# Moving the rounding of the feed-forward weights from GpSimd to ScalarE in a gated cross-attention kernel

## The reference

```python
x = x + jnp.tanh(g_xattn[0]) * xattn(layernorm(x), ctx, Wq, Wk, Wv, Wo, bo)      # 8 batches, 224 x 750, 8 heads
h = gelu(jnp.einsum('nd,edh->neh', layernorm(x), w1) + b1, approximate=False)    # 8 experts, 512 -> 1024
y = jnp.einsum('neh,ehd->ned', h, w2) + b2                                       # 1024 -> 512
x = x + jnp.tanh(g_ffn[0]) * (y * norm_g[:, None, None]).sum(axis=1)             # norm_g from the gate, top 1
```

## Time and profile before

| | |
|---|---|
| Median of 3 runs | 1889.43 us (1887.07 to 1889.46) |
| The profiled execution | 1885.9 us, its span 1884.1 us |
| TensorE busy | 1821.5 us, 97% |
| VectorE busy | 1328.9 us, 71% |
| GpSimd busy | 1184.9 us, 63% |
| ScalarE busy | 812.7 us, 43% |
| Mean granted TensorE clock | 0.99 of full speed |
| Feed-forward part | about 1200 us, 64 steps |

### The profile page before, as it was taken

The page is one execution under the profiler, slowest core; times in us unless marked ns, Lnnn a source line. Parts: engine busy times, 40 slices in busy tenths (PEclk is TensorE's granted clock), DMA queues, the critical chain, the costliest instruction groups (busy, mean ns, idle before and its releaser), DMA issues.

```text
span 1884.1 us, 32919 instructions
## 1 busy us (share of the span) xinstructions
PE 1821.5 (97%) x10360; PEld 1647.3 (87%) x10360; DVE 1328.9 (71%) x2247; ACT 812.7 (43%) x1570; POOL 1184.9 (63%) x901
## 2 busy tenths in 40 slices
PE   6999999999999869999999999999999999999998
PEld 6999999999999758888888888887888888888887
DVE  6777777777776776766766667579766676676667
ACT  4767666766766543332323323233223233232322
POOL 5525354352544468877777777867777777777742
PEclk9999999999999979999999999999999999999999
DMA  5011111021110213121121211213311112112111
GB/s 174 17 32 59 34 37 55 21 67 29 42 43 13 81 33 122 62 67 56 56 67 45 67 56 56 68 53 116 106 50 62 59 53 67 55 56 66 46 46 51
DMA packets 51804, 110.38 MB, mean 59 GB/s; under 512 B 12953, under 2 KB 25241, under 8 KB 51745
## 3 DMA queue, kind: packets, MB, share of 16 engines
q1 hardware_dynamic: 51744, 109.63, 18.2%
HBM read 98.61 MB, written 11.01 MB: 58 GB/s over the span
## 4 chain that ended last, share of the span: by engine, by line
PE 85%; DVE 9%; issue 3%; ACT 3%; DMA 0%; DVEq 0%; ACTq 0%; SPq 0%
PE bank L683 30%; PE scores L658 28%; PE bank L537 15%; PE scores L601 4%; PE bank L611 4%; PE bank L624 4%; DVE xs L777 1%; DVE neg_max L860 1%; DVE queries L841 1%; ACT queries L1057 1%; DVE acc L944 1%; PE bank L544 1%; DVE probsT L777 0%; PE scores L719 0%; DVE values L777 0%
## 5 line engine op out<-in xcount | busy, mean ns | idle before, releaser
L683 PE MATMUL bank<-w2s,hs 128*128 128x512 f32 x2688 | 621.8, 390 | 5.0 <-DVE acc L944 5.0
L683 PEld LDWEIGHTS bank<-w2s,hs 128*128 128x128 f32 x2688 | 504.3, 188 | 109.5 <-DVE acc L944 7.0
L658 PE MATMUL scores<-xs,w1s 128*128 128x448 f32 x2688 | 562.1, 368 | 4.2 <-DVE h_sum L923 4.2
L658 PEld LDWEIGHTS scores<-xs,w1s 128*128 128x128 f32 x2688 | 507.5, 189 | 49.0 <-issue 2.8
L923 DVE TENSOR_TENSOR h_sum<-scores,h_sum 128x448 f32<-128x448 f32 x448 | 267.2, 620 | 192.2 <-PE scores L658 191.8
L944 DVE TENSOR_TENSOR acc<-bank,acc 128x512 f32<-128x512 f32 x434 | 295.8, 687 | 123.8 <-PE bank L683 114.6
L1183 ACT ACTIVATE h_full<-h_sum,b1T 128x448 f32<-128x448 f32 x256 | 170.9, 668 | 316.9 <-DVE h_sum L923 306.6
L777 DVE TENSOR_TENSOR hs<-h_full,hs 128x448 fp32r<-128x448 f32 x256 | 237.0, 926 | 50.6 <-ACT hs L1184 50.6
L1057 ACT ACTIVATE h_sum<-scores 128x448 f32<-128x448 f32 x64 | 34.9, 545 | 489.9 <-PE scores L658 489.8
L1244 POOL TENSOR_SCALAR probs<-probs,row_inv 112x750 f32<-112x750 f32 x64 | 140.5, 2195 | 164.4 <-DVE row_inv L866 164.4
L1339 POOL CAST w1s<-w_stage 128x768 fp32r<-128x768 f32 x64 | 68.6, 1072 | 182.9 <-PE scores L658 182.9
(11 more groups left out here) (112 smaller groups left out, 2123.8 us busy)
## 6 DMA issues: line engine op xcount, KB each, us to landing
w_stage<-in_L_ffn_w SPq DMA_DIRECT2D x128, 512.0 KB, 3.5
ctx_raw<-in_ctx SPq DMA_DIRECT2D x8, 752.0 KB, 4.6
ctx_raw<-in_ctx SPq DMA_DIRECT2D x7, 748.0 KB, 4.6
xa<-in_x SPq DMA_DIRECT2D x16, 224.0 KB, 2.7
xres<-in_x SPq DMA_DIRECT2D x16, 224.0 KB, 2.7
x_scratch<-xres SPq DMA_DIRECT2D x16, 224.0 KB, 2.3
xt_scratch<-yT SPq DMA_DIRECT2D x16, 224.0 KB, 2.9
x_raw<-xt_scratch SPq DMA_DIRECT2D x4, 896.0 KB, 6.1
```

The source lines that it names most:

```text
L658: mm = pe.matmul(mb[BANK_OF[name]][:, 0:TH], w1s[j % 2][:, s, W_OF[name], kc, :], xs[:, i, m, kc, :], start=n == 0, stop=n == 5)
L683: mm = pe.matmul(bank[:, :], hs[j % 2][:, s, ht, t * P:(t + 1) * P], w2s[j % 2][:, m, ht, :], start=n == 0, stop=n == 5)
```

## The change

The three roundings of a step's weights go to ScalarE: two of w1 (`round_w1`, part 0 of 768 columns and part 1 of 1024) and one of w2 (`round_w2`). Part 0 for the next step stands behind `keep_p1`, before the first GELU; part 1 for the next step and w2's rounding for this step stand at the end of the step, in (0, 7, 3) behind the seven `round_x`. GpSimd keeps the four sums and the three subtractions, and waits for the roundings with a new semaphore w1_hi and with w2_hi. In the last batch's plan ScalarE does items W0.1, W0.3, W1.1 and W1.3; w2's rounding for step (0, 0, 0) stands between the plan and step (0, 0, 1). Nothing changes for TensorE, VectorE and SyncE.

```diff
--- before.py
+++ after.py
@@ -276,6 +276,7 @@
         b1_loaded, b2_loaded = sem("b1_loaded"), sem("b2_loaded")
         small_loaded, small_set = sem("small_loaded"), sem("small_set")
         w1_loaded, w1_step, w1_split = sem("w1_loaded"), sem("w1_step"), sem("w1_split")
+        w1_hi = sem("w1_hi")
         w2_loaded, w2_hi, w2_split = sem("w2_loaded"), sem("w2_hi"), sem("w2_split")
         mix_psum, p1_out, sum_out = sem("mix_psum"), sem("p1_out"), sem("sum_out")
         h_hi, h_act, h_split = sem("h_hi"), sem("h_act"), sem("h_split")
@@ -1066,7 +1067,15 @@
                     copy(probs[0:QT, i, :], probs[0:QT, i, :],
                          scale=row_inv[0:QT, i:i + 1]).then_inc(probs_scaled[qt], 1)
                     return
-                if kind in "RMDLAWOBGZ":
+                if kind == "W":
+                    if item[3] in (1, 3):
+                        if item[2]:
+                            act.wait_ge(in_psum["P"], number(("P", 0, H - 1), B - 1))
+                        else:
+                            act.wait_ge(in_psum["P"], number(("P", 0, G - 1), B - 1))
+                        round_w1((0, 0, item[2]), item[3] // 2)
+                    return
+                if kind in "RMDLAOBGZ":
                     return
                 if kind == "N":
                     name, g = WEIGHT_PIECES[item[2]]
@@ -1184,6 +1193,28 @@
                 act.activation(hs[j % 2][:, 0, ht, half * TH:(half + 1) * TH], src, ACT.Gelu,
                                bias=bias).then_inc(h_act, 1)
 
+            def round_w1(g, part):
+
+                p, e, j = g
+                if part == 0:
+                    act.wait_ge(w1_loaded, upto(16, g, 16))
+                    if not early(g, 2):
+                        act.wait_ge(mix_psum, upto(NM, g, -NM))
+                    alone(act, passed["act"])
+                    copy(w1s[j % 2][:, 0, 0:3], w1_stage[:, 1:4]).then_inc(w1_hi, 1)
+                else:
+                    act.wait_ge(w1_step, upto(4, g, 4))
+                    alone(act, passed["act"])
+                    copy(w1s[j % 2][:, 0, 3:7], w1_stage[:, 4:8]).then_inc(w1_hi, 1)
+
+            def round_w2(g):
+                p, e, j = g
+                if not early(g, 2):
+                    act.wait_ge(y_psum, upto(NM, g, -NM))
+                act.wait_ge(w2_loaded, upto(16, g, 16))
+                alone(act, passed["act"])
+                copy(w2s[j % 2][:, 0], w2_stage[:, :, :]).then_inc(w2_hi, 1)
+
             def hidden(g, i):
                 if i == 0:
                     keep_p1(g)
@@ -1200,8 +1231,11 @@
             def step(g):
                 p, e, j = g
                 closing = isinstance(e, int) and e == NE - 1
+                after = following(g)
                 for i in range(NM):
                     hidden(g, i)
+                    if i == 0 and after:
+                        round_w1(after, 0)
                     if closing and j == 1 and i in (0, 2):
                         half = i // 2
                         act.wait_ge(gate_psum, 2 * p + half + 1)
@@ -1215,7 +1249,11 @@
                 if at(g, (0, NE - 1, JS - 1)):
                     for i in range(NM):
                         round_x(1, i)
-
+                if after:
+                    round_w1(after, 1)
+                round_w2(g)
+
+            round_w2((0, 0, 0))
             steps(act, step, (0, 0, 1))
 
 
@@ -1324,7 +1362,11 @@
                 raw, w = w1_stage, w1s[j % 2]
 
                 def after(n):
-                    pool.wait_ge(w1_step, upto(6, g, n))
+                    pool.wait_ge(w1_step, upto(4, g, n))
+                    alone(pool, passed["pool"])
+
+                def rounded(n):
+                    pool.wait_ge(w1_hi, upto(2, g, n))
                     alone(pool, passed["pool"])
 
                 if k == 0:
@@ -1333,23 +1375,17 @@
                     pool.tensor_tensor(raw[:, 4], raw[:, 0], raw[:, 3], ALU.add).then_inc(w1_step, 1)
                     pool.tensor_tensor(raw[:, 6], raw[:, 1], raw[:, 0], ALU.subtract).then_inc(w1_step, 1)
                 elif k == 1:
-                    if not early(g, 2):
-                        pool.wait_ge(mix_psum, upto(NM, g, -NM))
-                        alone(pool, passed["pool"])
-                    pool.tensor_copy(w[:, 0, 0:3], raw[:, 1:4]).then_inc(w1_step, 1)
                     after(1)
                     pool.tensor_tensor(raw[:, 5], raw[:, 4], raw[:, 1], ALU.subtract).then_inc(w1_step, 1)
                 elif k == 2:
                     after(3)
+                    pool.tensor_tensor(raw[:, 7], raw[:, 2], raw[:, 5], ALU.subtract).then_inc(w1_step, 1)
+                elif k == 3:
+                    rounded(1)
                     pool.tensor_tensor(w[:, 1, 0:3], raw[:, 1:4], w[:, 0, 0:3].bitcast(F32),
                                        ALU.subtract).then_inc(w1_split, 1)
-                    after(4)
-                    pool.tensor_tensor(raw[:, 7], raw[:, 2], raw[:, 5], ALU.subtract).then_inc(w1_step, 1)
-                elif k == 3:
-                    after(5)
-                    pool.tensor_copy(w[:, 0, 3:7], raw[:, 4:8]).then_inc(w1_step, 1)
                 else:
-                    after(6)
+                    rounded(2)
                     pool.tensor_tensor(w[:, 1, 3:7], raw[:, 4:8], w[:, 0, 3:7].bitcast(F32),
                                        ALU.subtract).then_inc(w1_split, 1)
 
@@ -1357,11 +1393,6 @@
 
                 p, e, j = g
                 w = w2s[j % 2]
-                if not early(g, 2):
-                    pool.wait_ge(y_psum, upto(NM, g, -NM))
-                pool.wait_ge(w2_loaded, upto(16, g, 16))
-                alone(pool, passed["pool"])
-                pool.tensor_copy(w[:, 0], w2_stage[:, :, :]).then_inc(w2_hi, 1)
                 pool.wait_ge(w2_hi, upto(1, g, 1))
                 alone(pool, passed["pool"])
                 pool.tensor_tensor(w[:, 1], w2_stage[:, :, :], w[:, 0].bitcast(F32), ALU.subtract).then_inc(w2_split, 1)
```

## The result

The changed kernel takes 1899.43 us (median of 5 runs, 1899.15 to 1899.96), the kernel before 1888.39 us on the same chip: 1.0059 times as long (95% interval 1.0044 to 1.0074), a loss of 11.0 us. The prediction was 1895.3 us, a loss of 5.9.

A forecast was written before the change was run, and what follows sets the result against it. The prediction took TensorE alone to set an ordinary step, 18.04 us. Gates -6.0, turn +11.6 and seam +0.3 summed to +5.9 on the median 1889.43: 1895.3 us, range 1888.5 to 1903.

The forecast's parts named there:

- the two stalls that were named: At the turn: TensorE waits 5.6 us for w2 before (0, 7, 3)'s tiles, 6.9 for w1 before (1, 0, 1)'s products.
- the third rival: Turn dearer at +14.1 by VectorE's x2 wait and low clock, gates -4 as w1 is late: 1899.8 us, chance 0.15.
- Ordinary steps, 0: The 60 ordinary feed-forward steps stay at 18.04 us, set by TensorE alone, and cost nothing.
- The margin of 2.9: In an ordinary step w1's low part ends at 15.1 us; TensorE asks for w1 at 18.04.
- Gate steps, -6.0 predicted: Steps (0, 7, 2) and (1, 7, 2) each gain 3.0 us as VectorE no longer meets GpSimd; bounds 3 and 6.2.
- the old collision: Gate step: VectorE's L1018 took 2.42 us beside GpSimd's L1353; claimed to vanish because GpSimd is then free.
- The turn's first stall, +5.6 and +2.3: TensorE waits 5.6 us for w2, rounded behind x's seven pieces in (0, 7, 3); the lowered clock adds 2.3.
- The turn's second and third stall, +6.9, +2.3 and +0.9: Before (1, 0, 1)'s products TensorE waits 6.9 us for w1; clock adds 2.3, VectorE's late sum U2 after x2 0.9.
- What the turn gives back, -6.4: VectorE's arrears at the turn, 6.4 us in the kernel before, are caught up in TensorE's new, longer stall.
- The seam, +0.3: At the seam to attention, GpSimd's relief and ScalarE's added roundings nearly cancel: +0.3 us, bounds -1.5 and +1.5.
- The base: The +5.9 us was added to the median 1889.43 us, not the profiled 1885.9, giving 1895.3.

The follow-up runs named there:

- e1: Changed kernel with ScalarE's roundings of w1 for (1, 0, 0) and w2 ahead of the seven of x in (0, 7, 3): 1890.65 us.
- e2: Changed kernel with ScalarE rounding w1's second part for (1, 0, 1) ahead of the GELUs in step (1, 0, 0): 1891.23 us.
- e7: Changed kernel with the change undone at the turn alone, GpSimd rounding both w1 parts for (1, 0, 0) and (1, 0, 1) and w2 for (0, 7, 3): 1881.19 us.
- e9: Changed kernel with ScalarE rounding the second part of every w1 three times over: 1917.66 us.
- e10: Changed kernel with ScalarE rounding the second part of every w1 five times over: 2067.25 us.
- e4: Changed kernel with GpSimd's four subtractions that mix x of the second half issued in (0, 0, 2) and (0, 0, 3): 1897.28 us.
- e6: Changed kernel with SyncE issuing the w1 load for (1, 0, 2) behind the first two x2 load and output store pairs in (1, 0, 0): 1896.27 us.
- e3: Changed kernel with the edits of both e1 and e2: 1885.41 us.
- e12: As e11, but GpSimd keeps the order that the kernel before has in the last batch: 1897.92 us.
- e11: Changed kernel with GpSimd again rounding both w1 parts for (0, 0, 0) and (0, 0, 1) and w2 for (0, 0, 0): 1902.01 us.

## Why the prediction was right or wrong

**Sign and mechanism: right.** The loss is at the turn, and by the two stalls that were named: 5.67 us for w2 (5.6 in the prediction) and 6.3 for w1 (6.9; the bracket shows 6.10 of it). e1 and e2 each remove one of them by moving ScalarE's roundings alone, and e7 removes the turn's loss by giving five roundings back. The size is that of the third rival (the turn dearer at +14.1, gates -4, 1899.8), which had a chance of 0.15: turn +15.0, gates -4.1. Its reason holds for the turn; in the first gate step w1 was late by only 0.27, and the rest has another cause. The loss came out at 1.9 times the 5.9 forecast; that it lies inside the range owes more to the range's width, 14.5 us, than to the sum.

**Ordinary steps, 0: right.** 18.04 us, and no wait of TensorE in the 60 steps. The margin of 2.9 was in fact 3.1 (w1's low part ended at 1035.62, asked for at 1038.74), and e9 and e10 show that it is real and where it ends.

**Gate steps, -6.0 predicted, -4.1 measured.** The second one came nearly as worked out: its stage gives -2.90 against -3.0, the step alone 18.34 us against 21.15. In the first the step that failed is that with the old collision the stall goes. At the moment that I had named GpSimd was indeed free, and the seven-element operation (L1018 in the earlier trace rows) took 0.17 us. But I had counted w1's and w2's work and left out `mix_x`, which follows split_w2 in (0, 7, 1) and slid into (0, 7, 2) as GpSimd finished a step later. It held L998, an earlier operation of the gate's chain (128x56), for 2.12 us; the sum that TensorE needs (L924) stands behind it in VectorE's order, and TensorE waited 1.02. e4 moves the four subtractions, and the step comes out at 18.05 us. The old collision had gone, as predicted; one of the same kind had come.

**The turn's first stall, +5.6 and +2.3: right.** 5.67, and 11.98 instead of 9.53 us for the tiles, 2.45 lost to the clock. One reading behind its upper bound was wrong: the 1850 ns of VectorE's operation are a mean over eight, held and free ones mixed; where nothing holds it, it takes 1.08 us in the changed kernel's trace.

**The turn's second and third stall, +6.9, +2.3 and +0.9: mis-sized.** The wait was 6.3, the rest 6.8 instead of 3.2. The clock behind the second stall cost 2.8, not 2.3. The third stall was 2.24, not 0.9: the x2 tile came as late as worked out, but VectorE's two low parts behind it took 2.21 instead of 1.2 us, beside GpSimd's sums. And behind the third stall the clock fell again, a term that I had at nothing: 24 products took 6.59 instead of 4.86, 1.7 us. e6 removes the third stall and what followed it with SyncE's order alone, 3.4 us.

**What the turn gives back, -6.4: right in the changed kernel, and a warning for its repair.** VectorE's arrears vanished in the stalls. Where the stalls go they come back: 18.8 us of single savings became 13.9 in e3.

**The seam, +0.3: right in size** (+0.07), and e12 confirms that it is a null. Its bounds of -1.5 and +1.5 held for the change, but an order alone can do more there: e11 lost 3.2.

**The base.** I put the sum on the median; the 3.1 us by which the two traces differ ahead of the moved work belong to no term. Against the medians the forecast was 5.1 us short: 3.4 in the turn and 1.8 in the first gate step.

## What to carry to other kernels

Moving work to an idle engine costs nothing in the steady loop as long as its place in that engine's order leaves a margin (with 0.8 us left, e9 waited in ten of its ordinary steps). So look at the irregular places first: there other work already stands in the queue ahead of the moved work, and what used to be ready a step ahead is no longer. List everything on the engine that is relieved as well: when its schedule shifts, each remaining piece can land beside something new. And mend such a stall together with what it was hiding, in the order in which each comes to light; here four such edits made a loss of 11 us into a gain of 10.

## What the runs showed of the hardware

**A VectorE operation with two SBUF inputs waits while a GpSimd instruction runs, and once it waited for five.** The Trainium skill, page "SBUF — State Buffer", section "SBUF: two separate sides", says that whoever starts first has the pair for the whole instruction and the other blocks until it ends. The trace agrees in nearly every case: besides L998 (2.12 us) it shows it for the low parts `hs<-h_full,hs`, 0.62 us alone. In the changed kernel eleven of the 256 took over 0.9 us, and ten of these ended 0.48 us after the first GpSimd instruction that ended beside them, five of them although GpSimd went straight on. So in VectorE's row and GpSimd's two:

```profile
1236.14 2.68 DVE L778 TENSOR_TENSOR hs<-h_full,hs 128x448 fp32r<-128x448 f32 x1
```

```profile
1235.94 2.40 POOL L1389 TENSOR_TENSOR w1s<-w_stage,w1s 128x1024 fp32r<-128x1024 f32 x1 [8.26 <-ACT w1s L1058]
1238.31 2.80 POOL L1398 TENSOR_TENSOR w2s<-w_stage,w2s 128x1024 fp32r<-128x1024 f32 x1
```

The exception is the one at the seam. In e11 it took 6.66 us, through four whole instructions of GpSimd and the end of a fifth, and ended 0.47 us after GpSimd's first pause, which was 0.17 us long. In the changed kernel it ended 0.48 after GpSimd's next pause (706.82, the pause from 706.34), and in the kernel before 0.47 after it (703.02, from 702.55). Why it does not get its turn there between two instructions, as elsewhere, stays open.

**Idle times of 2 to 3 us lower the clock in some cases and not in others.** 2.24 us idle were followed by PEclk 0.50 from 1322 to 1325, and 3.20 us idle in e3 by 24 products in 6.69 instead of 5.0 us. But the 3.20 us in e1 were followed by 24 products in 5.13, with PEclk at 1.00 throughout, and 3.15 us in e9 by 24 in 5.22. Idle times of 0.66 to 0.85 left 24 products at 5.17 to 5.47. So the length of one idle time did not decide it here, and its price is not fixed.

**Executions differ early.** The two traces are 3.1 us apart at the second xa transposes, at 18.73 us in the one and 21.82 in the other, and at 653 and 656 they still are; between 41 and 650 us the distance stays within 3.1 to 3.3. Stages have to be compared from their own starts.
